# Side sums from f16 halves, and attention's first units without cleared rings, in a macaron transformer layer

## The reference

```python
x = x + 0.5 * ffn(layernorm(x), w_up, w_down)     # ternary weights, gelu, RMS norm before each linear
x = x + attention(layernorm(x), Wq, Wk, Wv, Wo)   # 16 heads of 64
x = x + 0.5 * ffn(layernorm(x), w_up, w_down)
```

```python
g = einsum('bld,lg->bgd', x, one_hot(arange(L) // 16))   # side sums
side_k, side_v = einsum(g, Wk), einsum(g, Wv)
probs = exp(logits - m) / (sum(exp(logits - m)) + exp(-m))   # m = max(logits, 0)
```

## Time and profile before

| | us |
|---|---|
| median of 3 runs | 2224.38 |
| lowest, highest | 2222.55, 2228.65 |
| the profiled execution, its own time | 2225.56 |
| its span, first to last instruction | 2222.3 |
| busy: PE, ACT, DVE, POOL | 2064.7, 1928.4, 1896.7, 1334.1 |
| first phase, attention, third phase begin at | 43, 330, 1969 |

### The profile page before, as it was taken

The page is one execution under the profiler, slowest core; times in us unless marked ns, Lnnn a source line. Parts: engine busy times, 40 slices in busy tenths (PEclk is TensorE's granted clock), DMA queues, the critical chain, the costliest instruction groups (busy, mean ns, idle before and its releaser), DMA issues. The chain is left out here.

```text
span 2222.3 us, 77396 instructions
## 1 busy us (share of the span) xinstructions
PE 2064.7 (93%) x30307; PEld 1595.4 (72%) x30307; DVE 1896.7 (85%) x4738; ACT 1928.4 (87%) x4150; POOL 1334.1 (60%) x1307
## 2 busy tenths in 40 slices
PE   0999987999999999999999999999999999979999
PEld 0677765777877777777777777777777777746666
DVE  6788877998889889988988899988898899867776
ACT  2888854999999899999999999999899999959997
POOL 1223224777777677777767777777677777722221
PEclk9999998999999999999999999999999999989999
DMA  3897854999999999999999999999999999959998
GB/s 142 153 165 158 160 97 70 166 170 172 172 168 170 150 150 175 173 167 177 171 162 145 176 169 171 175 171 164 143 172 169 176 171 170 168 85 176 180 176 183
DMA packets 1347900, 357.11 MB, mean 161 GB/s; under 512 B 1328080, under 2 KB 1346512, under 8 KB 1347536
## 3 DMA queue, kind: packets, MB, share of 16 engines
q1 hardware_dynamic: 1347536, 352.17, 99.1%
HBM read 14.68 MB, written 8.39 MB: 10 GB/s over the span
## 5 line engine op out<-in xcount | busy, mean ns | idle before, releaser
L928 POOL TENSOR_TENSOR probs_split<-probs,probs_split 128x512 f16<-128x512 f32 (+1 forms) x1026 | 1149.6, 1133 | 425.1 <-DVE probs_split L1265 297.3
L1254 DVE CUSTOM_DVE_ANT_0 probs<-score_ps,mask,neg_qk_scale 128x512 f32<-128x512 f32 (+1 forms) x1028 | 740.4, 720 | 93.0 <-PE score_ps L1032 91.6
L1193 ACT ACTIVATE probs<-probs,minus_max 128x512 f32<-128x512 f32 (+1 forms) x1027 | 718.7, 700 | 91.7 <-DVE minus_max L1254 85.7
L1051 PEld LDWEIGHTS y_ps<-v_parts,probsT 128*128 128x128 f16 x11931 | 467.2, 98 | 84.2 <-DMA probsT<-probs_split 12.2
L1051 PE MATMUL y_ps<-v_parts,probsT 128*128 128x64 f16 x11931 | 515.4, 193 | 9.6 <-DMA probsT<-probs_split 8.5
L1208 ACT ACTIVATE probs_split<-probs 128x512 f16<-128x512 f32 (+1 forms) x770 | 471.2, 612 | 21.9 <-DMA probsT<-probs_split 8.0
L1029 PE MATMUL score_ps<-k_parts,q_parts 64*128 64x384 f16 (+3 forms) x2604 | 380.4, 286 | 20.7 <-DVE minus_max L1254 18.9
L1032 PE MATMUL score_ps<-k_parts,q_parts 64*128 64x384 f16 (+3 forms) x2604 | 380.4, 286 | 0.0
L1029 PEld LDWEIGHTS score_ps<-k_parts,q_parts 64*128 64x128 f16 x2604 | 195.9, 94 | 138.1 <-DVE minus_max L1254 46.3
L961 PE MATMUL item_ps<-b_xT,wk_split 128*128 128x128 f16 x3168 | 221.8, 220 | 35.2 <-DVE b_xT L1246 33.3
L961 PEld LDWEIGHTS item_ps<-b_xT,wk_split 128*128 128x128 f16 x3168 | 182.2, 98 | 58.2 <-DVE b_xT L1246 38.8
(11 more groups left out here) (162 smaller groups left out, 3557.2 us busy)
## 6 DMA issues: line engine op xcount, KB each, us to landing
probsT<-probs_split SPq DMA_TRANSPOSE x1031, 4.0
out_x<-x_resident SPq DMA_DIRECT2D x64, 128.0 KB, 2.1
x_resident<-in_L_attn_x SPq DMA_DIRECT2D x56, 128.0 KB, 2.6
raw_up<-in_L_ffn_w_up SPq DMA_DIRECT2D x1, 1024.0 KB, 5.7
raw_down<-in_L_ffn_w_down SPq DMA_DIRECT2D x1, 1024.0 KB, 7.7
raw_q<-in_L_attn_Wq SPq DMA_DIRECT2D x1, 1024.0 KB, 9.6
raw_k<-in_L_attn_Wk SPq DMA_DIRECT2D x1, 1024.0 KB, 11.6
raw_v<-in_L_attn_Wv SPq DMA_DIRECT2D x1, 1024.0 KB, 13.4
```

The lines of the kernel that those rows point to most:

```text
L928: nc.gpsimd.tensor_tensor(parts_of[ring(at, v)][:, LO, low_columns(place_of(at, v))], probs[v % NBUF][:, cols], parts_of[ring(at, v)][:, H ...
L1051: last = nc.tensor.matmul(out, pt[ring(at, v)][:, low * a + t, :], vr[:, slot, b, h * DH:(h + 1) * DH], start=(n == 0), stop=(n == len(pas ...
L1193: nc.scalar.activation(probs[v % NBUF][:, cols], probs[v % NBUF][:, cols], ACT.Exp, bias=bias[:, j % 2, h:h + 1], scale=-1.0, accum_out=su ...
L1254: nc.vector.tensor_tensor_reduce(out=probs[v % NBUF][:, cols], in0=score_ps[v % NBUF][:, cols], in1=mask_of(at, v), scale=w.neg_qk_scale[: ...
```

## The change

It has two halves. In the first phase ACT makes the high half of each pair of second-normalised blocks (`second_high`, after the hidden layer of a tile's second and third step), POOL the low half (`second_low`, two in a row, between its roots), and PE's side sum takes f16 halves in two passes each, with the f16 group matrix. The f32 copy of that matrix is gone. Both outer phases now do the transposes and halves of the second pair of blocks ahead of the first `up`.

In attention, POOL's clears of the rings and the DMA queue's empty transposes are gone; a wait or a unit of probabilities by values that lies before unit 0 is skipped (`started`). Three small clears stay, and DVE clears half of `yT_parts`. The list PRE is in another order, and behind its sixth item PE makes the scores of units 0 to 3; DVE's maxima and ACT's exponentials of these units stand between the copies of the last seven items.

```diff
@@ first phase, gpsimd
+            def second_low(p):
+                pool.wait_ge(xn2hi_ready, p + 1)
+                nc.gpsimd.tensor_tensor(xn2_parts[LO][p % 2][:], xn2[p % 2][:], xn2_parts[HI][p % 2][:],
+                                        ALU.subtract).then_inc(xn2lo_ready, 1)
+
             rstd(0)
-            for t in range(NTILE + 1):
-                if t >= 1:
+            for t in range(NTILE + (2 if first else 1)):
+                if 1 <= t <= NTILE:
                     hidden_rms(t - 1)
                 if t + 1 < NTILE:
                     rstd(t + 1)
-                if first and t >= 1:
+                if first and t >= 2:
+                    second_low(2 * (t - 2))
+                    second_low(2 * (t - 2) + 1)
+                if first and 1 <= t <= NTILE:
                     rstd_second(t - 1)
@@ vector
-            nc.vector.tensor_copy(group32[:], w.group16[:]).then_inc(group_ready, 1)
             normalise_begin(0)
             normalise_end(0)
             normalise_end(1)
             x_lo(0)
+            x_lo(1)
...
-                    if t < NTILE:
+                    if 1 <= t < NTILE:
                         x_lo(2 * t + 1)
@@ tensor
-                pe.wait_ge(xn2_ready, 2 * p + 2)
+                pe.wait_ge(xn2lo_ready, p + 1)
                 if half == 0 and t >= 1:
                     pe.wait_ge(g_copied, t)
                 for k in range(KD):
                     for c in (2 * half, 2 * half + 1):
-                        last = nc.tensor.matmul(g_ps[:, k, c * GPB:(c + 1) * GPB], xn2[half][:, c % 2, k * P:(k + 1) * P],
-                                                group32[:], start=True, stop=True)
+                        for s in (HI, LO):
+                            last = nc.tensor.matmul(g_ps[:, k, c * GPB:(c + 1) * GPB],
+                                                    xn2_parts[s][half][:, c % 2, k * P:(k + 1) * P], w.group16[:],
+                                                    start=(s == HI), stop=(s == LO))
...
             turn(0)
+            turn(1)
             for n in STEPS:
                 t, i = divmod(n, TB)
                 if n < NBLK:
                     up(n)
-                if n == 0:
-                    turn(1)
@@ scalar
+            def second_high(p):
+                act.wait_ge(xn2_ready, 2 * p + 2)
+                if p >= 2:
+                    act.wait_ge(side_done, p - 1)
+                nc.scalar.activation(xn2_parts[HI][p % 2][:], xn2[p % 2][:], ACT.Copy).then_inc(xn2hi_ready, 1)
...
             x_hi(0)
+            x_hi(1)
             for n in STEPS:
                 t, i = divmod(n, TB)
                 if n < NBLK:
                     hidden(n)
-                if n == 0:
-                    x_hi(1)
                 if i >= 2 and t + 1 < NTILE:
                     x_hi(2 * (t + 1) + i - 2)
+                if first and i in (1, 2) and 2 <= t < NTILE + 2:
+                    second_high(2 * (t - 2) + i - 1)
@@ attention
-    CLEARED = 1 + NBUF + NPARTS + 1 + 3
+    CLEARED = 4
-    PRE = [(XTR, 0), (K0, 0), (K1, 0), (XTR, 1), (V0, 0), (V1, 0), (K0, 1), (K1, 1), (V0, 1), (Q0, 0), (Q1, 0),
-           (SV0, 0), (SK0, 0)]
+    PRE = [(XTR, 0), (Q0, 0), (K0, 0), (XTR, 1), (SK0, 0), (K0, 1), (V0, 0), (V0, 1), (K1, 0), (K1, 1), (Q1, 0),
+           (V1, 0), (SV0, 0)]
+    FIRST_SCORES = 6
@@ attention, sync
-            sp.wait_ge(cleared, CLEARED)
-            for n in range(NPARTS):
-                sp.dma_start_transpose(pt[n][:], parts_of[n][:].rearrange("p s n -> p (s n)")).then_inc(turned[n], 16)
-                sp.wait_ge(turned[n], 16)
@@ attention, gpsimd
-            nc.gpsimd.memset(vr[:, 2:], 0.0).then_inc(cleared, 1)
-            inverse_deviation(1)
-            for t in (*probs, *parts_of, yt):
-                nc.gpsimd.memset(t[:], 0.0).then_inc(cleared, 1)
             nc.gpsimd.memset(sums[:], 1.0).then_inc(cleared, 1)
             nc.gpsimd.memset(bias[:], 0.0).then_inc(cleared, 1)
             nc.gpsimd.memset(extra[:], 1.0).then_inc(cleared, 1)
+            inverse_deviation(1)
@@ attention, tensor
+                if not started(at, v):
+                    pe.sem_inc(pv_done.sem, 1)
+                    return
...
             for index, (kind, n) in enumerate(PRE):
+                if index == FIRST_SCORES:
+                    pe.wait_ge(lo_done, FIRST_SCORES)
+                    for v in range(0, SCORE_AHEAD, 2):
+                        scores(At(0, 0), v)
@@ attention, scalar
+            for index, (kind, n) in enumerate(PRE):
+                high(kind, index, pre_bank(index), n % 2, SIDE if kind in (SV0, SK0) else n)
+                if index == FIRST_SCORES:
+                    act.wait_ge(cleared, CLEARED)
+                if FIRST_SCORES <= index < FIRST_SCORES + EXP_AHEAD:
+                    v = index - FIRST_SCORES
+                    exponentials(At(0, 0), v)
+                    if v < SPLIT_AHEAD:
+                        split_high(At(0, 0), v)
@@ attention, vector
             nc.vector.memset(y_ps[1][:], 0.0).then_inc(y_cleared, 1)
+            nc.vector.memset(yt[:, :, 0:NPAIR // 2], 0.0).then_inc(cleared, 1)
...
+                if FIRST_SCORES <= index < FIRST_SCORES + SCORE_AHEAD:
+                    largest(At(0, 0), index - FIRST_SCORES)
                 low(kind, index, pre_bank(index), n % 2, SIDE if kind in (SV0, SK0) else n)
```

36 lines of the change are left out of this document (15 added, 21 removed).

## The result

The changed kernel takes 2202.48 us (median of 4 runs, 2200.54 to 2203.25) against 2225.04 us before in the same comparison: a ratio of 0.9895, 95% interval 0.9881 to 0.9910. That is 22.6 us less, where 15.2 were forecast; the time lies in the range, at its lower end.

| stretch | before | after | gained | forecast |
|---|---|---|---|---|
| up to the first copy of turned tokens (ACT) | 55.61 | 54.99 | 0.6 | 0 |
| from there to the copy of the 6th pair of blocks | 32.05 | 34.45 | -2.4 | 0 |
| rest of the first phase, 14 tiles in it | 242.36 | 229.40 | 13.0 | 5.2 |
| attention's first DVE instruction to the fifth maximum | 40.15 | 29.62 | 10.5 | 10.4 |
| rest of attention | 1605.8 | 1603.9 | 1.9 | 0 |

The account below looks back on a forecast made before the run. TensorE, without a gap in a tile, was taken to bound the first phase. Loop -5.6, phase's end +0.4, phases' start +0.4 and attention's start -10.4 make -15.2 us; by the runs' median 2209 us, range 2201 to 2217.

Parts of the forecast that it names:

- Part 1: First phase's side sums in f16: 9.8 us saved, less 4.2 of stalls, 5.6 gained in the loop.
- 0.058 each; 8 make 0.46: Price of an f16 side sum, from attention's nine loads in 0.52 us; saves 0.35 us per sum.
- the bound of 0.37: Most that one side sum could save, in us, if its loads take 0.055 each.
- The stall: PE waits for GpSimd's subtraction before a tile's even side sum: 0 to 0.65 us, taken as 0.3, 4.2 in 14 tiles.
- in between two of them: GpSimd's even subtraction gets between two of DVE's four normalisations, ends by 212.1, and PE loses nothing.
- a DVE that is busy without a gap in the tile: First-phase sign that the forecast is wrong, together with DVE being late with its subtraction of h.
- The phases' start: Turning the second pair before the first up product costs 0.4 us in the third phase, 0 in the first; at most 1.0.
- Attention's start: Clears removed and opening reordered: 10.6 - 0.7 + 0.5 = 10.4 us gained, from 7.5 to 13.
- the two stalls: Attention's normalisations of blocks 0 and 1 held up during GpSimd's clears: 4.9 and 5.7 us, together 10.6 gained.
- The upper bound of 13: Most, in us, that the forecast let the changes at attention's opening gain.
- attention gives more and the slack holds: Rival: loop gains 9.8 us, attention's opening 12.5, phase's end costs 0.4; 2202.5 us, chance 0.09.
- the late GpSimd: GpSimd's even subtraction, held up by DVE's four normalisations, comes up to 0.65 us too late for PE's side sum.

Follow-up runs that it names:

- e2: Changed kernel with 32 extra f16 matmuls of 64 columns ahead of the fourth pair's transposes in both outer phases; 2199.95 us, ratio 0.9887.
- e8: Changed kernel with every f16 matmul of the side sums done twice; 2204.76 us, ratio 0.9906.
- e4: e1 with both side sums of a tile in the tile's last step on TensorE; 2198.23 us, ratio 0.9875.
- e5: e1 with GpSimd's even subtraction held until both high halves are there, and both side sums behind the next tile's first up product; 2196.96 us, ratio 0.9878.
- e6: Changed kernel without GpSimd's subtractions, the low halves left at zero; 2195.14 us, ratio 0.9872.
- e7: Changed kernel with side sums from f32 tokens again, no casts and no subtractions; 2214.99 us, ratio 0.9958.
- e3: Kernel before with only the new order at the start of both outer phases; 2225.74 us, ratio 1.0006.
- e1: Changed kernel with the old order at the start of both outer phases; 2198.10 us, ratio 0.9877.
- e11: Changed kernel with six extra DMA-queue transposes, one after another, at attention's start; 2201.02 us, ratio 0.9904.
- e10: Changed kernel with the old order of attention's opening, still without the clears and empty transposes; 2203.15 us, ratio 0.9908.
- e9: Changed kernel with GpSimd's clears of v_parts and the ten ring buffers put back, without the empty transposes; 2210.24 us, ratio 0.9944.

## Why the prediction was nearly right

**Part 1, the loop, was mis-sized.** The step that failed is "0.058 each; 8 make 0.46", the price of a side sum of 8 matmuls. I divided the 0.52 us of nine weight loads by nine, but that row begins with a load that waits 0.2 us for its matmul. The matmuls of 64 columns start 0.029 apart, in the kernel before as in e2's fillers (32 in 1.10 us). Read so, the nearest row gives 8 x 0.029 = 0.23 and a saving of 0.58. With 8 columns they start 0.025 apart and make 0.20 (e8: 8 more cost 0.20). A side sum saves 0.61, not 0.35, and the bound of 0.37 I had set for it was wrong for the same reason. That alone is 28 x 0.61 = 17.1 in place of 9.8.

**The stall had the right size and the wrong cause.** I took 0.3 a tile for TensorE's wait ahead of the even sum; it is 15.48 - 15.17 = 0.31. But I took it as GpSimd being late for a gap in TensorE's program, held up by DVE's four normalisations. In fact GpSimd got in ahead of all four, sooner than in the case that I had put at nothing ("in between two of them"), and it was DVE that lost. e4 gave GpSimd a block's time more and the tile stayed; e5 and e6 took the collision away and it went. With TensorE's need down to 15.17, the 0.84 us that VectorE loses to GpSimd's subtraction makes VectorE the bound. I had listed "a DVE that is busy without a gap in the tile" as a sign of the forecast being wrong, and it is what came; the loop gained all the same. The rule of the Trainium skill that I weighed ("GPSIMD Engine Reference", section Specifications, the interfaces shared by the two engines) fits the rows in its pairings: the subtraction of h and the normalisations collide with GpSimd's subtraction, the operations on PSUM and the statistics don't. That the two take turns at instruction ends, and the 0.84 us, are what the rows add.

The traces have 13.2 us for the loop, up to the last block's Gelu, for a forecast 5.6. The phase's end behind it takes 17.45 us where it took 17.26, so 0.2 are lost where I had 0.4. Together that is the 13.0 of the table, and 12.5 by e7's median.

**The phases' start was mis-sized the other way**, 4.5 lost in the compared traces where I had said 0.4 and at most 1.0. The order itself costs the 0.4 a phase that I had for the third. What I left out is what a pause does behind itself: I had noted that PE "catches up" with ACT and did not ask how long it would then stand, nor what clock it would come back to. Such a fall costs 1.7 us. It came in 6 of 16 starts, so the changed kernel's profile, with both, shows more of it than most, and the medians leave the cost of the new starts open between nothing (e3) and 4.4 us (e1).

**Attention's start came out right as a sum, 10.5 for 10.4, with two errors that cancel.** The clears were worth 9.2 (forecast 10.6 - 0.7), the order 1.3 to 1.6 (forecast 0.5, bounds 2.5 either way). The empty transposes were free, as said. The 9.2 hold a term that the forecast lacks, the second fall of the clock, 1.6 us on twelve matmuls; so the two stalls by themselves gave less than I had for them. The upper bound of 13 was no sum either: 10.6 - 0.7 + 2.5 is 12.4.

**The rest of attention** gave 1.9 us in the compared traces. Its code and order are unchanged there. The stretch from the first normalised y to the third phase's first x_hi takes 1595.3 to 1602.3 us in the profiles of thirteen of the fourteen kernels here (before 1599.9, after 1598.2), and 1606.8 in e11's, and between the two compared traces the difference grows by steps of 0.2 to 0.6 us, some back and forth. So I count it as scatter of single executions, not as a gain. What makes these steps is open. Nor is it known why the first phase began 0.6 us earlier.

Of the rivals, "attention gives more and the slack holds" had the time (2202.5) but not the way: the slack didn't hold, and attention gave what the forecast said. Of the forecast's mechanisms, the shorter side sums and the stalls behind the clears came true in kind, the late GpSimd did not. Of its sizes two were off: by 7.6 us in the loop, and by -4.1 at the phases' start in the compared traces. That the time lies in the range is in part luck: the second error offset the first, and with the old starts (e1, 2198.1) the time would have been below the range.

## What to carry to other kernels

Take the pace of short matmuls from their starts, not from the length of a merged row divided by its count: such a row can begin with a wait, and a row of few instructions also holds the length of the last one. A row with more columns than yours bounds the cost from above and nothing from below. When an engine that has set the time gets lighter by more than its neighbour's slack, recompute each engine's busy time with the contention included, and take the largest; a wait that the profile then names may only be where the lighter engine's slack shows, and a run that moves the wait away tells the two apart. And when work is pulled ahead on TensorE, look at the pause that it leaves, and at the granted clock behind it.

## What the runs showed of the hardware

- An f16 matmul of 128x128 weights by 8 columns starts 0.025 us after the one before it, weight load included (after, e8); by 64 columns it was 0.029 (before, e2), and an f32 one by 8 columns 0.1 for each of two passes.
- After a pause of TensorE at the phases' start (2.10 to 2.30 us with the new starts) the granted clock fell to 0.50 for some 3 us in 6 of 16 cases in profiled executions, in the changed kernel's twice. The six all followed a pause of 2.29 or 2.30 us, but two pauses of that length (e6, e10) were followed by no fall, so the pause alone does not tell. In e2, with 1.18 us of pause behind the fillers, the clock held in both phases. Each fall cost 1.7 us.
- In attention's opening the granted clock fell to 0.50 for 6.8 us in the three kernels in which TensorE stood longest there behind GpSimd's clears (5.77 us before, 5.98 in e3, 3.47 in e9), and in no other; twelve f16 matmuls by 512 columns took 4.2 to 4.5 us, where the changed kernel took 2.8.
- GpSimd's and VectorE's instructions on SBUF waited for each other's end: a pair of normalisations took 1.57 us in place of 0.73 beside one subtraction. Beside a row of clears of 0.5 to 1 us, the same kind of instruction got in after 1.04 us in one kernel and only after all of them, 9.28 us, in another. GpSimd's subtraction beside VectorE's reads of PSUM and its statistics cost neither anything (e5, e6).
